# Routing, carried gate logits and the eighth expert's rows in a mixture-scan-mixture kernel

## What is computed

```python
logits = tokens @ gate_w                       # tokens: layernormed rows, E = 8 experts
probs = softmax(logits); expert_idx = argmax(probs)
pos = cumsum(one_hot(expert_idx)) - 1          # place within the expert, CAP = 160 kept
h = relu(einsum('ecd,edf->ecf', expert_input, w1))     # F = 512
expert_output = einsum('ecf,efd->ecd', h, w2)
out = einsum('tec,ecd->td', combine_weights, expert_output)   # row * its probability
...
x = x + 0.5 * ffn(layernorm(x))
x = x + scan(layernorm(x))                     # h = W h + B u;  y = C h + D u;  W circulant
x = x + 0.5 * ffn(layernorm(x))
```

## Time and profile before

| | us |
|---|---|
| median of three executions | 154.08 |
| profiled execution, as timed | 155.39 |
| profiled execution, span of its instructions | 153.2 |
| TensorE busy in the span | 135.3 |
| VectorE busy | 88.6 |
| ScalarE busy | 57.4 |
| GpSimd busy | 54.3 |
| mean granted TensorE clock, 1 being 2.4 GHz | 0.956 |

### The profile page before, as it was taken

One profiled execution on the slowest core, in us unless ns is written; L12 is line 12 of the kernel. 1 busy time (PEld: TensorE's weight loads), 2 busy tenths in 40 slices (PEclk: granted clock), 3 DMA queues, 4 the chain that ended last, 5 costly groups with the idle time before them and its releaser, 6 DMA issues.

```text
span 153.2 us, 2526 instructions
## 1 busy us (share of the span) xinstructions
PE 135.3 (88%) x784; PEld 103.0 (67%) x784; DVE 88.6 (58%) x384; ACT 57.4 (37%) x141; POOL 54.3 (35%) x87
## 2 busy tenths in 40 slices
PE   5897999999999969579999999999979899999810
PEld 2324476368999946239888778878874399899700
DVE  1078796954446541276877978999882243554220
ACT  2513410444583406055564656451100145742200
POOL 3440000777205777101311221122002777027770
PEclk9999995599999999999999999999996999999995
DMA  4999999111100111690011011101011111001110
GB/s 121 282 357 386 369 486 415 39 51 51 34 0 17 58 51 54 199 327 28 0 68 45 23 73 68 70 1 68 4 68 68 51 51 51 21 0 51 54 51 17
DMA packets 11308, 16.21 MB, mean 106 GB/s; under 512 B 1664, under 2 KB 6272, under 8 KB 11264
## 3 DMA queue, kind: packets, MB, share of 16 engines
q1 hardware_dynamic: 9504, 13.11, 24.2%
q0 software_dynamic: 1280, 2.62, 5.5%
q10 hardware_dynamic: 512, 0.33, 0.9%
HBM read 12.65 MB, written 5.51 MB: 118 GB/s over the span
## 4 chain that ended last, share of the span: by engine, by line
PE 43%; issue 12%; DVE 11%; DMA 11%; POOL 10%; ACT 5%; SPq 4%; POOLq 1%; DVEq 0%
PE pair L965 9%; PE pair L976 7%; PE pair L907 7%; DMA w1s<-w 5%; POOL xg L326 4%; PE pair L1043 4%; ACT u L466 3%; SPq L267 2%; PE pair L934 2%; POOL out L335 2%; PE pair L863 2%; POOL x_scratch L335 2%; PE pair L1034 2%; DMA x<-x_scratch 2%; DVE sstat L737 2%
## 5 line engine op out<-in xcount | busy, mean ns | idle before, releaser
L863 PE MATMUL pair<-warm_in,ones_bf 128*128 128x512 bf16 x70 | 20.3, 437 | 3.3 <-DMA x<-x_scratch 1.7
L976 PE MATMUL pair<-hT,w2s 128*128 128x160 f32 x128 | 20.4, 302 | 0.2 <-ACT hT L414 0.2
L965 PE MATMUL pair<-xcT,w1s 128*128 128x160 f32 x128 | 20.5, 303 | 0.0
L414 ACT ACTIVATE hT<-pair 128x320 f32<-128x320 f32 x32 | 14.0, 438 | 15.2 <-PE pair L965 13.5
L965 PEld LDWEIGHTS pair<-xcT,w1s 128*128 128x128 f32 x128 | 18.0, 190 | 1.2 <-ACT xcT L406 0.8
L976 PEld LDWEIGHTS pair<-hT,w2s 128*128 128x128 f32 x128 | 17.9, 190 | 0.4 <-issue 0.2
L326 POOL DMA_INDIRECT xg<-x,tok x10 | 10.2, 1020 | 19.9 <-issue 19.9
L863 PEld LDWEIGHTS pair<-warm_in,ones_bf 128*128 128x128 bf16 x70 | 7.5, 112 | 13.1 <-issue 4.7
L326 POOL DMA_INDIRECT xg<-out,tok x10 | 10.1, 1012 | 13.6 <-DVE tok L671 10.8
L678 DVE BATCH_NORM_STATS2 gstat<-xg 128x6 f32<-128x128 f32 x20 | 5.8, 290 | 14.2 <-DMA xg<-out,tok 10.3
L335 POOL DMA_INDIRECT x_scratch<-xnew,tok x10 | 9.9, 993 | 10.8 <-DVE xnew L715 9.0
(11 more groups left out here) (181 smaller groups left out, 245.0 us busy)
## 6 DMA issues: line engine op xcount, KB each, us to landing
xt<-x_turned SPq DMA_DIRECT2D x8, 256.0 KB, 5.9
w1s<-w SPq DMA_DIRECT2D x2, 1024.0 KB, 7.4
w2s<-w SPq DMA_DIRECT2D x8, 256.0 KB, 6.7
x<-x_scratch SPq DMA_DIRECT2D x8, 256.0 KB, 4.3
out<-x SPq DMA_DIRECT2D x8, 256.0 KB, 2.0
ce<-const_early ACTq DMA_DIRECT2D x1, 318.0 KB, 4.7
cl<-const_late SPq DMA_DIRECT2D x1, 256.0 KB, 5.5
xg<-x,tok POOLq DMA_INDIRECT x10, 2.5
```

Source lines behind the costliest of these rows:

```text
L414: nc.scalar.activation(hT[:, e % 2, half * HC:(half + 1) * HC, :], bank[4 + half][:, 0:HC * CAP] .rearrange("p (c s) -> p c s", c=HC), ACT ...
L863: M(bank[to][:, :], ones_bf[:, :], warm_in[:, :], start=True, stop=True)
L965: ins = M(bank[4 + half][:, c * CAP:(c + 1) * CAP], w1s[:, i, ch * P:(ch + 1) * P], xcT[:, i * CAP:(i + 1) * CAP], start=True, stop=True)
L976: ins = M(bank[6 + i % 2][:, 0:CAP], w2s[:, i, c, :], hT[:, i % 2, c, :], start=(c == 0), stop=(c == FC - 1))
```

## The change

Placing in the first mixture: `encode_four` makes `four_tok` for groups of four tiles, 80 columns of strip and tile; `place_four` multiplies them with 256 columns of `hot_place`, in eight matmuls; `own_places` keeps of each product the part in which both tiles are the same, and `place_own` sums it over the four tiles of a group in four matmuls. The centring of the weights stands round these in another order, eight and four warming matmuls before the slots are now six, and fourteen before the second mixture eleven. `index(0)` stands ahead of `lagged_inputs`.

`choose` writes `chosen` row by row and reads `key` with the stride. Square root and reciprocal are a logarithm and exponentials with a scale of -0.5 or 0.5, all from one table set, loaded once.

The copy of x to `x1_scratch` is eight DMAs, each behind a gather; both halves of w1 are loaded ahead of w2. x2 has 136 columns, the row and its eight logits. SyncE stores it as it is to a new `x2_scratch`, and its first 128 columns to the output. The second mixture gathers 136 columns and has no `l` steps on TensorE; its probabilities are made in two groups of five tiles. Its gathers wait for the stores to the scratch, its scatters for those to the output.

The eighth expert's second product takes the ReLU's output `hT` as weights and w2 as the moving operand, so its rows come out unturned: `t8` and `s8` are two halves of the 32 rows in tile 8, on each side of the turn `o7`, and `t9` is tile 9, in another bank. `d7` and its copy are gone.

```diff
-        x2 = sb("x2", [P, NT, D])
+        x2 = sb("x2", [P, NT, PITCH])
...
+        x2_dram = nc.dram_tensor("x2_scratch", [T, PITCH], F32, kind="Internal").ap()
...
+        def row_bank(i):
+
+            return 1 if i == NS - 1 else 2 + i % 2
...
-        pe_steps = steps("i0 x1 i1 x2 u0 i2 l0 l1 d0 i3 u1 i4 u2 i5 d1 i6 l2 l3 i7 l4 l5 u3 i8 l6 l7 i9 l8 l9 d2 "
-                         "u4 o0 o1 d3 u5 o2 o3 d4 o4 u6 o5 d5 u7 o6 d6 o7 d7 o8 o9")
-
-        dve_steps = steps("i0 i1 i2 i3 i4 d0 i5 i6 i7 i8 d1 i9 l0 d2 f0 o0 o1 d3 p5 "
-                          "o2 o3 d4 p6 o4 o5 d5 o6 d6 o7 d7 o8 o9")
-
-        act_steps = steps("i0 i1 u0 i2 i3 u1 i4 u2 i5 i6 i7 u3 i8 i9 g0 e0 u4 u5 u6 u7")
+        GROUPS = [[(0, NS)], [(0, NS // 2), (NS // 2, NS)]]
...
+        pe_steps = [steps("i0 x1 i1 x2 u0 i2 l0 l1 d0 i3 u1 i4 l2 u2 i5 l3 d1 i6 l4 l5 u3 i7 i8 l6 "
+                         "l7 i9 l8 l9 d2 u4 o0 o1 d3 u5 o2 o3 d4 o4 u6 o5 d5 u7 o6 d6 t8 o7 s8 o8 t9"),
+                    steps("i0 x1 i1 x2 u0 i2 u1 i3 d0 i4 u2 i5 d1 o0 i6 u3 o1 i7 d2 "
+                         "u4 o2 d3 i8 i9 u5 o3 o4 d4 u6 o5 d5 u7 o6 d6 t8 o7 s8 o8 t9")]
+
+        dve_steps = [steps("i0 i1 i2 i3 i4 d0 i5 i6 i7 i8 d1 i9 l0 f0 d2 "
+                         "o0 o1 d3 p5 o2 o3 d4 p6 o4 o5 d5 o6 d6 o7 o8 o9"),
+                    steps("i0 i1 i2 i3 i4 d0 l0 i5 f0 d1 i6 o0 i7 o1 d2 "
+                         "i8 o2 i9 d3 l1 o3 o4 f1 d4 o5 d5 o6 d6 o7 o8 o9")]
+
+        act_steps = [steps("i0 i1 u0 i2 i3 u1 i4 u2 i5 i6 "
+                         "i7 i8 i9 g0 u3 e0 u4 u5 u6 u7"),
+                    steps("i0 i1 u0 i2 u1 i3 i4 g0 u2 i5 e0 "
+                         "i6 u3 i7 u4 i8 i9 g1 u5 e1 u6 u7")]
...
                 sp.dma_start(w1s[:, h, :], w1[h].rearrange("e d f -> d e f")).then_inc(d_w1[i], 16)
+            for i in range(2):
                 for e in range(i * E // 2, (i + 1) * E // 2):
                     sp.dma_start(w2s[:, e, :, :], w2[e].rearrange("(c p) d -> p c d", p=P)).then_inc(d_w2[i], 16)
-            sp.dma_start(x1_dram, x_rows).then_inc(d_fill, 16)
-            sp.wait_ge(d_fill, 16)
+            for b in range(NB):
+                sp.wait_ge(d_gather[min(b + 3, NS - 1)], 16)
+                sp.dma_start(tiles(x1_dram, b), tiles(x_rows, b)).then_inc(d_fill, 16)
+            sp.wait_ge(d_fill, 16 * NB)
             sp.wait_ge(d_scatter, 16 * NS)
...
+            def store_rows(b):
+                sp.wait_ge(y_read, b + 1)
                 if b == LAST:
                     sp.wait_ge(x2_last, 1)
                 else:
                     sp.wait_ge(x2_r, b + 1)
-                sp.dma_start(tiles(out_rows, b), x2[:, b * TB:(b + 1) * TB, :]).then_inc(d_out, 16)
+                sp.dma_start(tiles(x2_dram, b), x2[:, b * TB:(b + 1) * TB, :]).then_inc(d_rows, 16)
+
+            def store_out(b):
+                sp.dma_start(tiles(out_rows, b), x2[:, b * TB:(b + 1) * TB, 0:D]).then_inc(d_out, 16)
+
+            for b in range(LAST - 1):
+                store_rows(b)
+                store_out(b)
+            store_rows(LAST)
+            store_rows(LAST - 1)
+            store_out(LAST - 1)
+            store_out(LAST)
...
+            nc.gpsimd.tensor_copy(token_half[:, :], token_code)
+            nc.gpsimd.tensor_copy(sum_strips[:, :], own_strip[0:NSTRIP * TB, :])
+            for g in range(NT // TB):
+                ins = nc.gpsimd.tensor_copy(strip_four[:, g, :, :], iota_strip.unsqueeze(2).broadcast_to([P, NSTRIP, TB]))
+            ins.then_inc(pool_set, 1)
             nc.gpsimd.tensor_copy(strip_no[:, :, :], iota_strip.unsqueeze(2).broadcast_to([P, NSTRIP, NT]))
-            nc.gpsimd.tensor_copy(token_half[:, :], token_code).then_inc(pool_set, 1)
...
+                    pool.wait_ge(d_rows, 16 * NB)
...
+                    pool.indirect_dma_start((xg[:, j, 0:D], xg[:, j, :])[n], None, (x_rows, x2_dram)[n],
...
                 if n == 0:
-                    pool.wait_ge(d_fill, 16)
+                    pool.wait_ge(d_fill, 16 * NB)
+                else:
+                    pool.wait_ge(d_out, 16 * NB)
...
-            nc.scalar.activation(table_load[:, 0:1], eps[:, 0:1], ACT.Sqrt)
+            nc.scalar.preload_act_table_set("natural_log_exp_and_others")
...
+                        g0, g1 = GROUPS[n][i]
+                        act.wait_ge(rated, n * NS + g1)
+                        nc.scalar.activation(gln[:, g0:g1], gmv[:, g0:g1, 1], ACT.Ln, bias=eps[:, 0:1]).then_inc(gln_r, 1)
+                        act.wait_ge(gln_r, group(n, i) + 1)
+                        nc.scalar.activation(grs[:, g0:g1], gln[:, g0:g1], ACT.Exp, scale=-0.5).then_inc(grs_r, 1)
                     elif kind == "e":
-                        act.wait_ge(lg_r, n + 1)
-                        nc.scalar.activation(pe_[:, :, :], lg[:, :, :], ACT.Exp).then_inc(pe_r, 1)
+                        g0, g1 = GROUPS[n][i]
+                        act.wait_ge(lg_r, group(n, i) + 1)
+                        nc.scalar.activation(pe_[:, g0:g1, :], lg[:, g0:g1, :], ACT.Exp).then_inc(pe_r, 1)
...
             def deviation(b):
                 act.wait_ge(svar, b + 1)
+                nc.scalar.activation(sln[:, b % 2, :], smv[:, b % 2, :, 1], ACT.Ln, bias=eps[:, 0:1]).then_inc(sln_r, 1)
+                act.wait_ge(sln_r, b + 1)
+                if 2 <= b < 4:
+                    act.wait_ge(u_half, b - 1)
+                nc.scalar.activation(srs[:, b % 2, :], sln[:, b % 2, :], ACT.Exp, scale=-0.5).then_inc(srs_r, 1)
                 if b >= 4:
                     act.wait_ge(y_read, b - 3)
-                nc.scalar.activation(ssd[:, b % 4, :], smv[:, b % 2, :, 1], ACT.Sqrt, bias=eps[:, 0:1]).then_inc(ssd_r, 1)
+                nc.scalar.activation(ssd[:, b % 4, :], sln[:, b % 2, :], ACT.Exp, scale=0.5).then_inc(ssd_r, 1)
...
             deviation(0)
             normalise(0)
+            copy_uT(0)
             deviation(1)
-            copy_uT(0)
+            turned_part(0)
             normalise(1)
-            turned_part(0)
...
-                return V.tensor_tensor(chosen[n][k][:, :, t0 - first:t0 - first + wd].rearrange("p e t -> p t e"),
-                                       key[:, ts, :], top_key[:, ts].unsqueeze(2).broadcast_to([P, wd, E]), ALU.is_equal)
+                return V.tensor_tensor(chosen[n][k][:, :, t0 - first:t0 - first + wd],
+                                       key[:, ts, :].rearrange("p t e -> p e t"),
+                                       top_key[:, ts].unsqueeze(1).broadcast_to([P, E, wd]), ALU.is_equal)
...
+            def encode_four():
+
+                def by_four(a):
+                    return a.rearrange("p (g t) -> p g t", t=TB).unsqueeze(2).broadcast_to([P, NT // TB, NSTRIP, TB])
+
+                link(V.tensor_tensor(four_strip[:, :, :, :], by_four(split_i[:, 1, :]), strip_four[:, :, :, :], ALU.is_equal))
+                V.tensor_tensor(four_tok[:, :, :, :], four_strip[:, :, :, :], by_four(token_half[:, :]), ALU.mult)
+
+            def own_places():
+
+                dve.wait_ge(four_placed, 1)
+                V.tensor_tensor(spread[:, :, :],
+                                bank[7][0:NSTRIP * TB, 256:256 + SW * TB].rearrange("p (s t) -> p s t", t=TB),
+                                own_tile[0:NSTRIP * TB, :].unsqueeze(1).broadcast_to([NSTRIP * TB, SW, TB]),
+                                ALU.mult).then_inc(spread_r, 1)
...
@@ -721,10 +799,11 @@
             dve.wait_ge(pool_set, 1)
             mark(0, 0)
             number(0, 0)
-            encode(0, 0)
+            encode_four()
             encode_place(0, 0)
+            own_places()
+            index(0)
             lagged_inputs()
-            index(0)
             carried_table()
             powers(ct, st, 0, 5)
...
-                dve.wait_ge(ssd_r, b + 1)
+                dve.wait_ge(srs_r, b + 1)
                 if b >= 2:
                     dve.wait_ge(u_r, b - 1)
                 if 2 <= b < 4:
                     dve.wait_ge(u_half, b - 1)
-                link(V.reciprocal(srs[:, b % 2, :], ssd[:, b % 4, :]))
...
-                V.tensor_tensor(lgs[:, b * TB:(b + 1) * TB, :].rearrange("p (h r) e -> p h r e", h=2),
+                V.tensor_tensor(x2[:, b * TB:(b + 1) * TB, D:PITCH].rearrange("p (h r) e -> p h r e", h=2),
...
+            def place_four():
+
+                for part_no, (t0, t1) in enumerate(hot_parts(0, 0)):
+                    pe.wait_ge(hot, part_no + 1)
+                    for t in range(t0, t1, TB):
+                        ins = M(bank[7][0:NSTRIP * TB, 256:256 + SW * TB],
+                                four_tok[:, t // TB, :, :].rearrange("p s t -> p (s t)"), hot_place[:, :, t:t + TB],
+                                start=(t == 0), stop=(t == NT - TB))
+                ins.then_inc(four_placed, 1)
+
+            def place_own():
+
+                pe.wait_ge(spread_r, 1)
+                for t in range(TB):
```

(34 more changed lines are left out.)

110 lines of the change are left out of this document (62 added, 48 removed).

## The result

The changed kernel takes 150.36 us (median; the kernel before, beside it, 154.21): a ratio of 0.974, with a 95% interval of 0.970 to 0.978. That is 3.85 us less, where 6.1 were forecast. The time lies inside the forecast's range, 2.4 us above its value. The change was measured again later (after_again): all ten executions together have a median of 151.0, 0.4 above the upper end of that range.

A forecast was written before the change was run, and what follows sets the result against it. TensorE's placing and half-clock centring were taken to bound the first stage, TensorE and GpSimd the mixtures' second halves, a TensorE-ScalarE ring the scan. Gains 3.4 + 0.3 + 2.4 = 6.1 us took 154.1 to 148.0; range 146.6 to 150.6.

The forecast's parts named there:

- Term 1: First mixture's routing: cheaper `chosen`, earlier rank and wider placing matmuls issue the first gather at 24.8 instead of 26.53.
- Term 2: First mixture: with the clock at 2.4 GHz TensorE is ready when tiles land; first scatter 47.2 to 43.8.
- it lands at 39.2: First mixture: the tenth gather, issued at 36.8, has its tile landed at 39.2, setting the last logits and first scatter.
- Term 3: First mixture's scatters keep their 1.30 pitch, tenth 59.21 to 55.5; waiting for the copy gives back 0.3, bounds 0 and 1.4.
- rival 2: First mixture: the copy is late or its pieces slow the gathers; 0.8 to 1.4 lost, time 149.1; chance 0.12.
- the worthless tail: First mixture: the eighth expert's new tail gains nothing, its last row being ready over a microsecond before GpSimd's turn.
- Term 4: Scan and second routing: small savings less a wait at the scan's start gain a net 0.3, bounds -0.3 and 0.8.
- the ring: Scan: the TensorE and ScalarE loop per sequence keeps its 5.0 us period despite more small ScalarE operations.
- Term 5: Second mixture: logits carried with the rows and the eighth expert's shorter tail gain 2.4.
- Rival 1: First mixture: the clock is at 1.2 GHz while the first experts run; 1.4 to 2.6 lost, time 150.0; chance 0.17.
- Rival 3: Second mixture starts cold with fewer warming matmuls; 1.5 lost, time 149.5; chance 0.09.
- Rival 4: Second mixture: 544-byte rows cost two transfers, gathers come 2.3 apart; 6.8 added, time 154.8; chance 0.04.

The follow-up runs named there:

- before_again: The kernel before, unchanged, measured and profiled once more: median 154.25 us.
- copy_early: Changed kernel with the copy's eight pieces issued once both layers' weights have landed, without waiting for gathers: 153.87 us.
- copy_whole: Changed kernel with the copy as one transfer queued right behind the second layer's weights, as in the kernel before: 152.89 us.

## Why the prediction was right, and where its size was off

**Term 1 (first gather 24.8): right.** 24.8 to 25.3 in the ten profiles with the new placing, early copies and all. `chosen` takes 0.41 (0.35 taken, 0.72 before), and encode_four its 0.49 twice. Against the kernel before it is 1.5 and not 1.7: the rank matmuls start at 16.58 and not 16.3, and from the last hot_place to the gather 1.1 are gained, as said.

**Term 2 (first scatter 43.8, gain 3.4): the step that failed first.** The sum set the first scatter against 47.23, a profile in which the centring ran at half clock. That stretch is not the usual one. In the usual execution (before_again) TensorE already waits for the first tile, and the first scatter is at 45.77. I had the warning: the text itself says that the profiled execution was 155.39 while the median was 154.08, and then took the gain worked out in the one from the other. (Its "0.9 over the span" sets the median beside the span of that other execution, whose own time is 2.2 over its span.) That is 1.46 of the 3.4. The clock's gain is real, but only in executions in which the old placing brought it down: 22 of 81, as far as two profiles and the mean clocks tell. The second step that failed is "it lands at 39.2": the tenth tile landed at 40.09, beside the copy. With it o0 is at 43.32 and not 42.1; the other 0.3 is the chain behind that tile, 3.18 long here as in before_again, for 2.9 in the sum.

**Term 3 (0.3 for the new wait, bounds 0 to 1.4): mis-sized, inside its bounds at the wrong end.** From o0 to the first scatter 2.21, where before_again has 1.61: 0.6 for the wait. Each piece took 3.0 to 4.1 us to land, where the lower end had the 1.98 of a store. With the 0.66 more from the first expert to o0 (13.52 against 12.86), the copy in pieces costs 1.26 of the 1.5 that term 1 wins. That the 0.66 is the copy's is argued: the order of steps changed too, but TensorE turns the tenth tile 3.19 behind its issue where before_again has 2.56, which is 0.63 of it. The first mixture gains 0.6 in place of 3.4 (0.36 comes from scatters that follow more closely, 11.62 against 11.98; there the ninth had waited 0.61 for its row). This is rival 2, to which I gave 0.12; it gave 149.1, and the price it named (0.8 to 1.4) is what was measured. The copy could not simply be moved: copy_early and copy_whole show that elsewhere it costs more. The rule that I cited, that each DMA engine takes turns between queues by whole packets, stands in the Trainium skill, "DMA: Bandwidth & Descriptors", under "Queues, rings and completion order" and not under the heading that the prediction names. What I drew from it, that the gathers' time would stay nearly as it was, the trace does not bear out: median landing went from 2.6 to 3.2 and, beside all eight pieces at once, to 4.2 with a worst of 6.3. Whether the turns or something else holds the gathers up, no run separates. The scatters' pitch, 1.29, and the worthless tail in this mixture were right.

**Term 4 (0.3): wrong by 0.4, inside its bounds.** From the tenth scatter to the second gather 58.41 became 58.53. From the tenth scatter to vq(0) and from vq(7) to the gather 0.22 and 0.23 were gained; the ring kept its pace (30.3 from vq(1) to vq(7) in both); but normalise(1) behind vq(0) cost 0.57, where 0.35 was taken.

**Term 5 (2.4): right, a little small.** 2.8 against the first profile and 3.0 against the usual one: logits with their order of steps 2.54 (2.5 forecast, from which I took 0.6 for new waits that cost about nothing net, though u1 does wait 0.57 for its tile), tail 0.43. Last three scatters 1.3 apart, as said.

**The sum.** With both profiles from usual executions, the rows give 154.2 - 3.5 = 150.7, which is 0.1 over the range. The forecast's 6.1 was too large by 2.8 in the first mixture and 0.4 in the scan, and too small by 0.6 in the second mixture. That the time lies inside the range is in part luck: the first four executions gave 150.36, the six of after_again 151.69, and the range's upper end had been opened for rivals, not for a profile that was slower than usual.

**The rivals.** Rival 1 (half clock in the first experts) did not occur in any profile of the changed kernel, but copy_early shows its mechanism at work once TensorE has idled 2.8 us for a tile. There the rule of the Trainium skill, "TensorE: Matmul & The Clock Gate", "HAM oscillation — how this bites in real kernels", that idle gaps bring the clock down, agrees with the trace. In the earlier trace rows the clock fell while TensorE was busy for all of each microsecond from 18 on, which that rule does not cover. Rival 3 (second mixture starts cold) occurs in some executions and costs 1.4 (1.5 said). Rival 4 is false: the gathers of 544-byte rows are issued 1.3 apart (115.68 to 127.50 in nine steps).

## What to carry to other kernels

Before a gain is read off a profile, ask whether that execution is a usual one: if its time is off the median by more than the spread of the others, find the stretch that differs before a term rests on it. Where a stage is entered by gathers, a bulk transfer beside them can cost more in their latency than it saves by being done (copy_early, copy_whole). Sent sooner, it delayed the first tiles, and an engine that idles for a tile can lose its clock as well.

## What was not expected of the hardware

The granted clock falls in some executions of a program and not in others, at the same place: in the centring behind 32 matmuls of 20 columns (1.00 or 0.50, worth 1.46 us at the first scatter), behind a wait of 2.3 us ahead of the scan (14 matmuls in 3.20 or 4.88 us), and at the first tiles of the second mixture (28.4 or 29.8 us). What tells the executions apart stays open. Rows of 544 bytes cost a gather 0.1 us at most: GpSimd spends 1.00 us on each, and they land after 2.6 (median), where those of 512 bytes in the second mixture of before_again took 2.5.
